# Context as host-turned tiles, a narrower inverse, new attention places, later shared weights

## The reference

```python
def attention(query, key, value, mask, wq, wk, wv, wo):
    Q = rope((query @ wq) in heads); K = rope((key @ wk) in heads); V = (value @ wv) in heads
    scores = where(mask == 0, -1e9, Q K^T / sqrt(32))
    return (softmax(scores) V) @ wo
def ffn(x):                      # router: top 2 of 8 experts, F=256, and a shared expert of 512
    out = sum over the chosen experts of rw * ((silu(x Wg[e]) * (x Wu[e])) Wd[e])
    return out + (silu(x Sg) * (x Su)) Sd
x = x + attention(layernorm(x), ctx, ctx, mask, wq, wk, wv, wo)
x = x + ffn(layernorm(x))
```

## Time and profile before

| | |
|---|---|
| time, median of 3 runs | 1487.92 us (1486.22 to 1488.44) |
| the profiled execution's own time | 1489.88 us |
| its span, first to last instruction | 1488.1 us |
| mean granted TensorE clock | 0.984 |
| PE, DVE, ACT, POOL busy | 95%, 66%, 59%, 37% of the span |

### The profile page before, as it was taken

How to read it: one execution, slowest core, us unless ns; L and a number is a source line. 1 busy time by engine, 2 the same in 40 slices (tenths; PEclk the granted TensorE clock), 3 DMA queues, 4 the chain that set the end, 5 groups by cost and what they waited for, 6 DMA issues and landing times.

```text
span 1488.1 us, 28824 instructions
## 1 busy us (share of the span) xinstructions
PE 1415.5 (95%) x8362; PEld 1105.6 (74%) x8362; DVE 984.0 (66%) x2692; ACT 874.4 (59%) x1994; POOL 549.7 (37%) x670
## 2 busy tenths in 40 slices
PE   5698999999999999999788899999999999999997
PEld 4576777777777877778565677777777888888885
DVE  4688889889888888888675666666663343334332
ACT  2589989888888888888894222222222343444342
POOL 2343331423414234232432342222223555455553
PEclk9799999999999999999998999999999999999999
DMA  5334445454554545444544232222246787886652
GB/s 166 105 108 133 119 150 148 123 163 124 146 151 124 160 129 148 146 118 136 170 126 166 96 80 86 85 86 85 86 128 186 186 191 182 259 194 112 107 85 37
DMA packets 141464, 198.26 MB, mean 133 GB/s; under 512 B 34944, under 2 KB 72576, under 8 KB 141315
## 3 DMA queue, kind: packets, MB, share of 16 engines
q1 hardware_dynamic: 119954, 158.33, 35.3%
q0 software_dynamic: 17952, 33.64, 12.3%
q10 hardware_dynamic: 3408, 4.46, 0.9%
HBM read 97.10 MB, written 69.35 MB: 112 GB/s over the span
## 4 chain that ended last, share of the span: by engine, by line
PE 83%; issue 4%; ACT 4%; DVE 3%; POOL 2%; DMA 2%; SPq 1%; another core or an unknown queue 0%; POOLq 0%; DVEq 0%; ACTq 0%
PE psum L641 15%; PE psum L1407 12%; PE psum L1409 11%; PE psum L1408 11%; PE psum L750 7%; PE psum L731 7%; PE psum L686 4%; PE psum L687 4%; PE psum L688 4%; PE psum L1474 2%; ACT a_probs L544 2%; PE psum L656 2%; PE psum L1503 1%; PE psum L1403 1%; ACT a_probsT L550 1%
## 5 line engine op out<-in xcount | busy, mean ns | idle before, releaser
L544 ACT ACTIVATE a_probs<-a_probs,a_low 128x512 f32<-128x512 f32 x512 | 371.1, 727 | 75.0 <-DVE a_low L895 73.8
L895 DVE CUSTOM_DVE_ANT_0 a_probs<-psum,a_bias 128x512 f32<-128x512 f32 x512 | 347.3, 686 | 90.3 <-PE psum L731 86.1
L641 PE MATMUL psum<-a_ident,a_probs 128*128 128x128 f32 x2048 | 312.9, 276 | 15.0 <-ACT a_probsT L550 7.1
L641 PEld LDWEIGHTS psum<-a_ident,a_probs 128*128 128x128 f32 x2048 | 245.0, 141 | 83.2 <-ACT a_probs L544 29.4
L731 PE MATMUL psum<-a_kT,a_q_stack 128*128 128x512 f32 x512 | 248.6, 487 | 11.0 <-issue 5.7
L550 ACT ACTIVATE a_probsT<-psum 128x512 f32<-128x512 f32 x344 | 203.6, 592 | 26.7 <-PE psum L641 26.6
L1276 POOL DMA_INDIRECT out<-b_y,b_pairs_sb x71 | 113.2, 1595 | 149.3 <-DMA out<-b_y,b_pairs_sb 89.1
L1712 DVE SCALAR_TENSOR_TENSOR b_v_hidden<-b_v_hidden,psum 128x256 f32<-128x256 f32 x71 | 29.9, 422 | 165.7 <-ACT b_v_hidden L1372 88.9
L471 POOL CAST a_w_hi<-a_w_raw 128x256 fp32r<-128x256 f32 x96 | 38.4, 400 | 267.5 <-DMA w_halves<-a_w_lo 263.5
L901 DVE COPY a_probsT<-psum 128x512 f32<-128x512 f32 x168 | 115.3, 686 | 18.4 <-PE psum L641 18.0
L750 PE MATMUL psum<-a_probsT,a_v 128*32 128x512 f32 x1024 | 118.2, 603 | 0.2
(11 more groups left out here) (206 smaller groups left out, 3165.8 us busy)
## 6 DMA issues: line engine op xcount, KB each, us to landing
b_w<-w_halves SPq DMA_DIRECT2D x16, 1536.0 KB
a_q_stack<-a_qT_hi SPq DMA_DIRECT2D x256, 64.0 KB, 2.0
a_q_stack<-a_qT_lo SPq DMA_DIRECT2D x256, 64.0 KB, 2.0
w_halves<-a_w_hi SPq DMA_DIRECT2D x96, 128.0 KB, 2.0
w_halves<-a_w_lo SPq DMA_DIRECT2D x96, 128.0 KB, 1.8
a_x_in<-in_x SPq DMA_DIRECT2D x32, 256.0 KB, 2.9
a_ctx_in<-in_ctx SPq DMA_DIRECT2D x32, 256.0 KB, 3.0
a_x_res<-in_x SPq DMA_DIRECT2D x32, 256.0 KB, 3.0
```

The source lines that it names most:

```text
L544: nc.scalar.activation(probs[:, h % 2, t], probs[:, h % 2, t], ACT.Exp, bias=low[:, h % H, t:t + 1], scale=-1.0, accum_out=total[:, h // G ...
L641: last = nc.tensor.transpose(out[:, P * i:P * (i + 1)], src(i), identity[:])
L895: nc.vector.tensor_tensor_reduce(probs[:, h % 2, t], psum[:, t % 2], bias[:, t], 1.0, HUGE, ALU.add, ALU.min, low[:, h % H, t:t + 1]).then ...
```

## The change

The host hands over the context as tiles that are turned already: tile n holds, for each of the 128 rows of a quarter c of D, the 128 tokens. The load's size stays the same. TensorE's turning of the context, ScalarE's copy of it and the tile `ctxT` are gone; `project_kv` reads `ctx_in` itself, and the load of a later context tile now waits for `kv_filled` in place of `ctxT_filled`. The reciprocals lie in a tile of 8 columns, so that their transposes have 8 columns of weights and fill 8 partitions; the zeros are now written once into `inverseT`, and the matmul of `spread` has the shape that it had. All tables of places are new, and 17 instead of 21 of the 64 tiles of probabilities are copied by VectorE. In `last`, SP issues Sg at u = 43, Su at u = 46 and the constants at u = 53, and GpSimd splits them at u = 51, 56 and 58. The words of the change also name six middle batches that are written out; the bodies of the diff run as often as before. The tile `inverse_hl` has another address.

```diff
-DVE_EVACUATES = ((2,), (0, 1), (), (1, 3), (3,), (2,), (), (1, 3), (0, 1), (0,), (2,), (0,), (1, 3), (0, 1), (3,), (0, 3))
+DVE_EVACUATES = ((0, 1), (0, 1), (0, 3), (3,), (1,), (), (), (0,), (1,), (1,), (), (), (2,), (0, 2, 3), (2,), (3,))
...
 PE_AT = {
-    1: (('out', -1),), 2: (('inverse', -1),), 4: (('spread', -1),), 5: (('ctxT', 0), ('xT', 0)), 9: (('q', 0),), 11: (('q', 1),), 12: (('kv', 0),),
-    13: (('q', 2),), 14: (('q', 3),), 15: (('xT', 1),), 16: (('qT', 2),), 17: (('out', 0),), 18: (('ctxT', 1), ('inverse', 0)), 19: (('q', 4),),
-    20: (('spread', 0),), 21: (('q', 5),), 22: (('xT', 2), ('q', 6), ('q', 7)), 23: (('kv', 1),), 24: (('q', 8), ('kT', 0)),
-    25: (('ctxT', 2), ('q', 9), ('q', 10)), 26: (('q', 11),), 27: (('xT', 3), ('qT', 3)), 29: (('q', 12), ('q', 13)), 30: (('q', 14),),
-    31: (('q', 15),), 33: (('out', 1),), 34: (('inverse', 1),), 36: (('wo', 0), ('spread', 1)), 37: (('kv', 2),), 38: (('wo', 1), ('wo', 2)),
-    39: (('wo', 3), ('kT', 1)), 41: (('ctxT', 3),), 43: (('wo', 4), ('wo', 5)), 44: (('wo', 6), ('kT', 2)), 46: (('kv', 3),),
-    47: (('wo', 7), ('qT', 4)), 49: (('out', 2),), 50: (('inverse', 2), ('kT', 3)), 51: (('wo', 8),), 52: (('wo', 9), ('spread', 2)),
-    53: (('wo', 10),), 54: (('wo', 11),), 58: (('wo', 12),), 60: (('wo', 13), ('wo', 14), ('wo', 15)), 63: (('qT', 5),),
+    1: (('out', -1),), 3: (('inverse', -1),), 5: (('kv', 0), ('xT', 0), ('spread', -1)), 8: (('q', 0),), 10: (('q', 1),), 12: (('q', 2),),
+    13: (('q', 3),), 15: (('xT', 1),), 16: (('qT', 2),), 17: (('out', 0),), 19: (('inverse', 0),), 20: (('q', 4),),
+    21: (('q', 5), ('q', 6), ('spread', 0)), 22: (('q', 7), ('xT', 2)), 23: (('kv', 1),), 24: (('kT', 0), ('q', 8)), 25: (('q', 9), ('q', 10)),
+    26: (('q', 11),), 27: (('xT', 3),), 28: (('qT', 3),), 29: (('q', 12), ('q', 13)), 30: (('q', 14), ('q', 15)), 33: (('out', 1),),
+    35: (('wo', 0), ('inverse', 1)), 37: (('wo', 1), ('spread', 1)), 38: (('wo', 2),), 39: (('kT', 1), ('wo', 3)), 41: (('kv', 2),), 43: (('wo', 4),),
+    44: (('kv', 3),), 46: (('wo', 5),), 47: (('wo', 6), ('qT', 4)), 49: (('out', 2),), 50: (('kT', 2), ('wo', 7)), 51: (('inverse', 2),),
+    52: (('wo', 8),), 53: (('wo', 9), ('spread', 2)), 54: (('wo', 10),), 55: (('kT', 3), ('wo', 11)), 57: (('wo', 12),), 58: (('wo', 13),),
+    60: (('wo', 14), ('wo', 15)), 63: (('qT', 5),),
 }
...
 SP_AT = {
...
+    3: (('stack', (1, 0)), ('ctx', 2)), 5: (('stack', (1, 1)), ('save', 0)), 7: (('stack', (1, 2)), ('save', 1)), 8: (('x', 2),),
+    30: (('stack', (3, 0)), ('save', 5), ('load', 4)), 31: (('save', 6), ('load', 5)), 32: (('load', 6),), 33: (('ctx', 3),),
+    34: (('stack', (3, 1)),), 36: (('stack', (3, 2)), ('stack', (3, 3)), ('store', 0)), 38: (('save', 7),), 39: (('residual', 1),), 40: (('ctx', 4),),
+    41: (('load', 7), ('residual', 2)), 42: (('stack', (4, 0)), ('x', 4)), 44: (('stack', (4, 1)),), 45: (('save', 8),), 47: (('x', 5),),
+    49: (('store', 1),), 50: (('stack', (4, 2)), ('residual', 3)), 51: (('ctx', 5),), 55: (('stack', (4, 3)), ('store', 2), ('save', 9), ('load', 8)),
+    56: (('load', 9),), 60: (('save', 10),), 62: (('save', 11), ('load', 10)), 63: (('load', 11),),
...
 POOL_AT = {
-    2: (('root', 0),), 4: (('piece', 0), ('root', 1)), 5: (('qsum', 0),), 7: (('piece', 1),), 8: (('k', 0), ('root', 2)),
-    13: (('low', -1), ('piece', 2), ('qsum', 1)), 14: (('root', 3),), 19: (('k', 1), ('piece', 3)), 26: (('qsum', 2),), 28: (('piece', 4),),
-    29: (('low', 0), ('piece', 5)), 30: (('qsum', 3),), 37: (('piece', 6),), 42: (('k', 2), ('piece', 7)), 45: (('k', 3), ('low', 1)),
-    49: (('piece', 8),), 50: (('piece', 9),), 55: (('piece', 10),), 61: (('low', 2),), 63: (('piece', 11),),
+    4: (('root', 0),), 7: (('piece', 0), ('piece', 1)), 9: (('root', 1),), 11: (('low', -1),), 12: (('piece', 2),), 13: (('qsum', 0),),
+    16: (('k', 0),), 17: (('root', 2),), 21: (('piece', 3),), 22: (('qsum', 1),), 25: (('root', 3),), 26: (('qsum', 2),),
+    27: (('piece', 4), ('piece', 5), ('low', 0)), 29: (('k', 1),), 32: (('qsum', 3),), 37: (('piece', 6), ('piece', 7)), 41: (('k', 2), ('k', 3)),
+    43: (('low', 1),), 46: (('piece', 8),), 47: (('piece', 9),), 59: (('piece', 10), ('low', 2)), 60: (('piece', 11),),
 }
...
-    inverse_hl = sb("inverse_hl", [P, TT, P], F32R)
+    inverse_hl = sb("inverse_hl", [P, TT, 2, GH], F32R)
...
         def load_ctx(b, t):
-            wait_count(sp, s["ctxT_filled"], b * TT + (TT + t - 1))
+            wait_count(sp, s["kv_filled"], b * TT + (TT + t - 1))
             sp.dma_start(ctx_in[:, t % 2], ctx_rows[b * TT + (TT + t)]).then_inc(ctx_loaded[t % 2], 16)
...
-                if u == 4 and part == "last":
+                if part == "last" and u in (43, 46, 53):
...
-                if part == "last" and u in (7, 11, 39):
+                if part == "last" and u in (51, 56, 58):
...
-        def turned_ctx(part, b, t):
-            act.wait_ge(s["ctxT_filled"], upto(b, "ctxT", t))
-            nc.scalar.activation(ctxT[:], psum[:, ring_bank(part, "ctxT", t)], ACT.Copy).then_inc(s["ctxT_ready"], 1)
...
-            nc.scalar.activation(inverseT[:], psum[:, ring_bank(part, "inverse", g)], ACT.Copy).then_inc(s["inverseT_ready"], 1)
+            nc.scalar.activation(inverseT[0:2 * GH], psum[0:2 * GH, ring_bank(part, "inverse", g)], ACT.Copy).then_inc(s["inverseT_ready"], 1)
...
-        def turn_ctx(part, b, t):
+        def project_kv(part, b, t):
             pe.wait_ge(ctx_loaded[t % 2], b * 32 + (48 + 16 * (t // 2)))
-            four(in_ring(part, b, "ctxT", t), lambda i: ctx_in[:, t % 2, P * i:P * (i + 1)], ident).then_inc(s["ctxT_filled"], 1)
-
-        def project_kv(part, b, t):
-            pe.wait_ge(s["ctxT_ready"], upto(b, "ctxT", t))
             out = in_ring(part, b, "kv", t)[:, 0:2 * KV]
             for c in range(DC):
-                last = nc.tensor.matmul(out, ctxT[:, P * c:P * (c + 1)], wkv[:, c], start=(c == 0), stop=(c == DC - 1))
+                last = nc.tensor.matmul(out, ctx_in[:, t % 2, P * c:P * (c + 1)], wkv[:, c], start=(c == 0), stop=(c == DC - 1))
             last.then_inc(s["kv_filled"], 1)
 
...
-                last = nc.tensor.transpose(out[:, P * t:P * (t + 1)].bitcast(F32R), inverse_hl[:, t], ident_r[:])
+                last = nc.tensor.transpose(out[0:2 * GH, P * t:P * (t + 1)].bitcast(F32R), inverse_hl[:, t].rearrange("p r h -> p (r h)"), ident_r[:])
...
-        sp.wait_ge(attention["ctxT_filled"], TILES)
+        sp.wait_ge(attention["kv_filled"], TILES)
         sp.dma_start(raw[:, 0], sg.rearrange("(c p) n -> p c n", p=P)).then_inc(s["raw_in0"], 16)
+        yield
         sp.wait_ge(attention["q_filled"], TILES)
         sp.wait_ge(attention["kv_filled"], TILES)
         sp.wait_ge(attention["q_added"], TILES)
         sp.dma_start(raw[:, 1], su.rearrange("(c p) n -> p c n", p=P)).then_inc(s["raw_in1"], 16)
+        yield
         sp.dma_start(router_raw[:], wr.rearrange("(c p) n -> p c n", p=P)).then_inc(s["const_in"], 16)
...
+        if name == "ctx_1024":
+            a = a.reshape(B * TT, P, DC, P).transpose(0, 3, 2, 1)
```

More of the change, by code:

```diff
@@ L51 @@
 }
 SP_AT = {
-    1: (('stack', (1, 0)), ('ctx', 2)), 3: (('x', 2),), 7: (('stack', (1, 1)),), 10: (('save', 0),), 11: (('stack', (1, 2)), ('stack', (1, 3))),
-    13: (('x', 3),), 14: (('save', 1), ('load', 0)), 15: (('stack', (2, 0)), ('load', 1)), 17: (('residual', 0),), 21: (('load', 2),),
-    22: (('stack', (2, 1)), ('stack', (2, 2)), ('stack', (2, 3))), 23: (('save', 2), ('save', 3)), 24: (('stack', (3, 0)),), 25: (('residual', 1),),
-    26: (('load', 3),), 27: (('save', 4),), 28: (('stack', (3, 1)),), 29: (('x', 4),), 30: (('load', 4),), 34: (('ctx', 3),),
@@ L57 @@
-    36: (('save', 5), ('stack', (3, 2)), ('load', 5)), 37: (('x', 5),), 38: (('store', 0),), 39: (('save', 6), ('load', 6)),
-    41: (('save', 7), ('stack', (3, 3)), ('load', 7), ('residual', 2)), 42: (('ctx', 4),),
-    44: (('save', 8), ('stack', (4, 0)), ('stack', (4, 1)), ('store', 1)), 47: (('ctx', 5),), 48: (('load', 8),), 49: (('stack', (4, 2)),),
-    51: (('store', 2),), 54: (('residual', 3),), 56: (('stack', (4, 3)),), 58: (('save', 9),), 59: (('load', 9), ('load', 10)), 61: (('save', 10),),
@@ L61 @@
-    62: (('save', 11), ('load', 11)),
+    3: (('stack', (1, 0)), ('ctx', 2)), 5: (('stack', (1, 1)), ('save', 0)), 7: (('stack', (1, 2)), ('save', 1)), 8: (('x', 2),),
+    10: (('stack', (1, 3)),), 14: (('x', 3), ('load', 0), ('load', 1)), 19: (('stack', (2, 0)), ('save', 2), ('load', 2)), 21: (('stack', (2, 1)),),
+    24: (('stack', (2, 2)), ('stack', (2, 3)), ('save', 3)), 27: (('load', 3), ('residual', 0)), 28: (('save', 4),),
+    30: (('stack', (3, 0)), ('save', 5), ('load', 4)), 31: (('save', 6), ('load', 5)), 32: (('load', 6),), 33: (('ctx', 3),),
@@ L74 @@
     "wkv": 205824, "ident": 207872, "k_cos": 208384, "k_sin": 208640, "k_rot": 208896, "low": 209152, "total": 209408, "inverse": 209664,
```

(18 more changed lines are left out.)

37 lines of the change are left out of this document (18 added, 19 removed).

## The result

The changed kernel takes 1480.7 us (median of 6 runs, 1478.3 to 1482.3), the kernel before in the same session 1488.6 (6 runs): a ratio of 0.995, 95% interval 0.9938 to 0.9962. It is 7.9 us faster, where 16.6 were forecast. The time lies in the forecast's range, but less than half of the gain came. The two profiled executions differ by 9.3 us (1489.88 and 1480.61), so a comparison of their parts adds up to 1.4 us more than the medians give.

A forecast was written before the change was run, and what follows sets the result against it. TensorE was taken to bound the middle batches, ScalarE and waits more the outer two. Savings of 14.1 + 0 + 1.0 + 5.5 - 4.0 = 16.6 us gave 1473.3 profiled, 1471.3 as median; range 1462 to 1482.

The forecast's parts named there:

- the new places: Middle batches: the new order was to cut 2.35 us of waits a batch by 0.45 us.
- Context not turned: Middle batches: four groups of context transposes go from TensorE, 1.76 us saved a batch.
- inverses: Middle batches: transposes of the inverses with 8-wide weights, 0.04 us saved a group, 0.15 a batch.
- `start`: Start of the kernel: its chain does not wait for the context, so 0 saved.
- `first`: First batch: TensorE's turning counts in its first half only, 1.0 us saved (0 to 2).
- `last`: Last batch: later shared-weight loads free SP for the second head's `stack`, 5.0 us, plus 0.5 for SP's later backlog.
- the 2 us that the engines were taken to have in hand: `last`: of 7 us lateness of the second head's `stack`, perhaps 2 were taken as cost-free, leaving 5.0 saved.
- The end: Before the feed-forward phase: GpSimd's splits delay piece 10 by 3.6 us, plus 0.4 for the clock, 4.0 lost (0 to 7).
- SP's queue: Rival, chance 0.06: context loads waiting for `kv` delay `stack` on SP; at 3.5 us a batch, 1495 us.
- VectorE as the bound: Rival, chance 0.13: VectorE (u = 17 to 33) or ScalarE becomes the limit; 1.0 us a batch saved, 1482 us.
- A split on GpSimd did hold VectorE: Rival, chance 0.08: a cast of the inverses in `last` waits for a GpSimd split, 4.5 us more, 1476 us.
- the last rival: No change that can be told, chance 0.03: 1.5 us new waits a batch against 1.9 saved, 1487 us.

The follow-up runs named there:

- E3: Changed kernel with the shared weights' loads (SP, u = 4) and splits (GpSimd, u = 7, 11, 39) of `last` back where they were before; 1483.0 us.
- E8: Changed kernel with only SP's shared-weight loads put back to u = 4 of `last`, GpSimd's splits left late; 1482.4 us.
- E1: Changed kernel with SP issuing the loads of weight pieces 2 and 3 earlier, at u = 5 and 7 instead of 14; 1474.4 us.
- E2: Changed kernel with GpSimd splitting piece 2 behind `root` 2 instead of ahead of it; 1474.3 us.
- E9: E6 plus, in `last`, SP's piece 9 save and piece 10 load before x2's third store, small loads at u = 57, Su's second half-split behind piece 11; 1467.1 us.
- E4: Changed kernel with all places, evacuations and shared-weight times of the kernel before, keeping only the host-turned context and narrow inverses; 1476.2 us.
- E5: E4 with the shared weights' loads and splits at the change's late places in `last`; 1478.7 us.
- E6: Changed kernel with both the early loads of pieces 2 and 3 and piece 2 behind `root` 2; 1472.8 us.
- E7: E1 with, in `last`, SP's shared-weight loads at u = 40, 44, 57 and GpSimd's splits at u = 48, 52, 58; 1473.8 us.
- E10: E6 with, in `last`, SP's piece 9 save and piece 10 load ahead of x2's third store and six small loads at u = 57; 1470.9 us.

## Why the prediction was wrong

**The step that failed: the new places, 0.45 us less of waits a batch.** The prediction priced the places by ScalarE and VectorE alone. It went through SP's queue for the context and `stack`, but never through GpSimd's, where the change put piece 2, which waits for a transfer, ahead of `root` 2, and piece 1 ahead of `root` 1. The waits of a middle batch did not fall by 0.45 but rose by some 0.7: 1.91 us of work went by the prediction's prices and 1.23 of time (1.6 in E3 and E8, so some 0.3 at the least). With that queue mended the same places save 2.3 us a batch (E1, E2) and 2.7 (E9), for 2.35 forecast. Term: 14.1 us forecast, 7.4 measured (9.4 and 9.5 in E3 and E8), 13.7 with E1's edit.

**Context not turned, 1.76 us a batch; inverses, 0.15.** Right in size: E4, which has these alone, saves 1.5 of 1.9. The price of a group is 0.44 us in the chain; the inverses' group fell by 0.06, not 0.04. By the Trainium skill, "TensorE: Matmul & The Clock Gate", "LDWEIGHTS (loading the stationary operand)", the prediction had estimated 0.1 as the other value: the trace lies between, nearer to 0.04. The recorded weight load fell from 141 to 84 ns; the estimate's 7 ns for 8 columns is not what the record shows.

**`start` 0.** Right within 0.3 us. **`first`, 1.0 saved.** Wrong: 0.1 longer. Its sections show a gain behind u = 8 and a loss of 2.4 us ahead of it, where TensorE waits 2.8 us for the low half of q (2.2 before) and the granted clock is 0.66 against 0.84 in 54.8 to 68.6 us. E4, with the old places, shows 1.5 of these 2.4. No run changed this by itself; its cause is read, not tested.

**`last`, 5.5 saved.** Right in size, 4.6 measured, and the mechanism is shown for SP: 5.5 us in E8. But the 4.6 hide two things. In the new order the early splits on GpSimd would have cost 2.6 more; and the new order with early weights makes `last` 3.5 us longer than before (90.9 for 87.4, E3). The change needs its own late weights, in the old order they are a loss (E5). No run shows the 2 us that the engines were taken to have in hand.

**The end, 4.0 lost.** Right in place and near in size: the load of x2 came 4.2 us later counted from u = 63, the rest 2.4 (3.3 against E3). The splits are only one of two causes; the other is SP's six small issues and the slow store of x2 ahead of piece 10's load, which the prediction had put under the splits' cover (it counts seven late issues there; Sg, Su and six small ones are eight). Each is enough by itself: in E6, where the splits ended 2.1 us ahead of piece 10, SP's part alone held it, and in E7 and E10, where its load was issued 3.8 and 5.0 us ahead of u = 63, the splits alone did, until 5.5 and 2.7 us behind it.

**The rivals.** SP's queue was named with the right kind of harm, a queue in order behind a wait, but at the context and with the wrong sign for the whole. VectorE as the bound is out by E1 and E2, and in the changed kernel it is busy for 22.7 of 26.1 us in u = 17 to 33 of the second middle batch. A split on GpSimd did hold VectorE once, in the cast of 1.54 us beside su_lo, where TensorE then waited 2.9 us for the inverses; E3, without the split there, shows a wait of 2.4 us at the same place, so it is worth some 0.5 us and not 4.5. The time of the last rival, 1487, does not follow from its terms: 0.4 us a batch saved gives 1485.5, and less with the other terms; nothing hangs on it.
